# Gathering the first three tiles inside the routing block of a mixture-of-experts kernel, with part of the multiplications of zeros moved from the experts' block to the end of the routing

## The reference

```
x = x + 0.5 * ffn(layernorm(x))
x = x + attn(layernorm(x))
x = x + 0.5 * ffn(layernorm(x))
```

```
router_logits = x_flat @ gate_w                      # (2048, 8)
topk_w, topk_idx = top_k(softmax(router_logits), 2)
topk_w = topk_w / sum(topk_w)
x_rep_sort = x_flat[sort_idx // 2]                   # rows sorted by expert
h = silu(ragged_dot(x_rep_sort, w1)) * ragged_dot(x_rep_sort, w3)   # 256 -> 896
out_sort = ragged_dot(h, w2)                         # 896 -> 256
out = sum over the two experts of a token, weighted by topk_w
```

## Time and profile before

| what | value |
|---|---|
| median of 3 runs | 2851.32 us (2850.3 to 2853.34) |
| the profiled execution's own time | 2851.57 us |
| its span, first to last instruction | 2849.9 us |
| mean granted TensorE clock | 0.977 |
| TensorE (PE) busy | 2682.9 us, 94% |
| VectorE (DVE) busy | 1883.0 us, 66% |
| ScalarE (ACT) busy | 1357.7 us, 48% |
| GpSimd (POOL) busy | 692.1 us, 24% |
| DMA | 488.70 MB, mean 171 GB/s |

### The profile page before, as it was taken

The page is one execution under the profiler, slowest core; times in us unless marked ns, Lnnn a source line. Parts: engine busy times, 40 slices in busy tenths (PEclk is TensorE's granted clock), DMA queues, the critical chain, the costliest instruction groups (busy, mean ns, idle before and its releaser), DMA issues. The chain is left out here.

```text
span 2849.9 us, 63072 instructions
## 1 busy us (share of the span) xinstructions
PE 2682.9 (94%) x22216; PEld 2218.0 (78%) x22217; DVE 1883.0 (66%) x3550; ACT 1357.7 (48%) x4371; POOL 692.1 (24%) x969
## 2 busy tenths in 40 slices
PE   8999996748999999999999999999999997999997
PEld 7999995426777777777777777777777776899997
DVE  4111114979999999999999999999987544311111
ACT  1111112526666666666676666666665553011111
POOL 1222222421222222231322222231321111122221
PEclk8999998969999999999999999999999999999999
DMA  8777762555564554555554554546453322777674
GB/s 279 214 225 217 225 181 65 196 161 155 162 190 142 176 165 153 179 162 167 159 180 145 182 162 156 176 146 193 145 169 104 103 67 80 262 216 226 216 227 132
DMA packets 412292, 488.70 MB, mean 171 GB/s; under 512 B 215488, under 2 KB 295872, under 8 KB 412032
## 3 DMA queue, kind: packets, MB, share of 16 engines
q1 hardware_dynamic: 397056, 464.86, 50.4%
q0 software_dynamic: 14976, 20.46, 4.8%
HBM read 348.64 MB, written 138.67 MB: 171 GB/s over the span
## 5 line engine op out<-in xcount | busy, mean ns | idle before, releaser
L555 PE MATMUL f_ps_up<-f_xgT,f_w_up 128*128 128x128 f32 x4368 | 500.8, 275 | 0.0
L555 PEld LDWEIGHTS f_ps_up<-f_xgT,f_w_up 128*128 128x128 f32 x4368 | 494.4, 192 | 0.2
L624 DVE TENSOR_TENSOR f_hT<-f_hT,f_ps_up 128x512 f32<-128x512 f32 (+1 forms) x156 | 96.9, 621 | 503.4 <-ACT f_hT L603 503.4
L1574 DVE SCALAR_TENSOR_TENSOR at_qk<-at_bank,at_taps_qk,at_qk 128x510 f32<-128x510 f32 (+2 forms) x384 | 282.0, 744 | 36.1 <-ACT at_qk L1448 26.9
L1574 DVE SCALAR_TENSOR_TENSOR at_vT<-at_bank,at_taps_v,at_vT 128x510 f32<-128x510 f32 (+2 forms) x384 | 280.4, 744 | 35.9 <-ACT at_vT L1455 26.8
L603 ACT ACTIVATE f_hT<-f_ps_up 128x512 f32<-128x512 f32 (+1 forms) x156 | 84.9, 544 | 428.3 <-PE f_ps_up L555 428.3
L1844 POOL TENSOR_SCALAR at_small<-at_small 128x4 f32<-128x4 f32 x64 | 15.2, 238 | 1105.8 <-ACT at_squares L1482 1105.8
L1250 PE MATMUL at_bank<-xnT,at_w_qk 128*128 128x512 f32 x512 | 256.5, 625 | 11.7 <-DVE at_qk L1574 7.1
L519 POOL DMA_INDIRECT sums<-f_y,f_row_of x78 | 123.8, 1587 | 534.2 <-DVE f_y L630 534.2
L566 PE MATMUL f_ps_y<-f_w_down,f_hT 128*128 x1092 | 248.8, 379 | 3.8 <-DVE f_hT L624 3.8
L1275 PE MATMUL at_bank<-at_w_vz,xnT 128*128 128x256 f32 x1024 | 243.6, 381 | 8.5 <-DVE at_vT L1574 8.5
(11 more groups left out here) (230 smaller groups left out, 5535.1 us busy)
## 6 DMA issues: line engine op xcount, KB each, us to landing
f_w_up<-in_L_ffn_w_dram SPq DMA_DIRECT2D x156, 896.0 KB, 6.4
at_steps_e<-steps_kept SPq DMA_DIRECT2D x64, 512.0 KB, 6.9
mt_kept<-at_mt_made SPq DMA_DIRECT2D x64, 512.0 KB, 4.3
pt_kept<-at_pt_made SPq DMA_DIRECT2D x64, 512.0 KB, 3.1
at_mt<-mt_kept SPq DMA_DIRECT2D x64, 512.0 KB, 4.1
at_pt<-pt_kept SPq DMA_DIRECT2D x64, 512.0 KB, 4.6
qk_kept<-at_qk SPq DMA_DIRECT2D x64, 256.0 KB, 2.6
ks_kept<-at_ks_made SPq DMA_DIRECT2D x64, 256.0 KB, 2.7
```

The costliest lines, as they stand in the source:

```text
L555: last = te.matmul(ps_up[hf][w][:, at:at + P], w_up[b][:, w, k, P * j:P * j + P], xgT[b][:, k, :], start=(k == 0), stop=(k == KD - 1))
L624: v.tensor_tensor(part, part, ps_up[hf][1][:, 0:P * (high - low)], ALU.mult).then_inc(h_ready, 1)
L1574: ins = v_.scalar_tensor_tensor(out=dst[:, :, back:], in0=src[:, :, 0:SEQ - back], scalar=taps[:, 3 - back:4 - back], in1=dst[:, :, back:] ...
```

## The change

- The buffers `xg`, their semaphores `rows_loaded` and `gather` are defined for the whole of `build_ffn`. POOL issues the gathers of the first three tiles at the end of its program in the routing block, after waits for `rows_stored` (64) and for the second count of `table_ready`.
- TensorE multiplies zeros 9 times at the end of the routing block, and 6 times where it did 14 times at the start of the experts' block.
- In the experts' block POOL begins with the gather of tile 3. The order of its later gathers and stores is as before.

```diff
@@ -176,6 +176,15 @@
+        xg = [r.sb(f"xg{b}", [P, D]) for b in range(RING)]
+        rows_loaded = [r.dma_sem(f"rows_loaded{b}") for b in range(RING)]
+
+        def gather(t):
+            nc.gpsimd.indirect_dma_start(
+                out=xg[t % RING][:], out_offset=None, in_=rows_in,
+                in_offset=bass.IndirectOffsetOnAxis(ap=token_of[:, t:t + 1], axis=0),
+            ).then_inc(rows_loaded[t % RING], 16)
@@ -302,6 +311,7 @@
                     last.then_inc(tokens_summed, 1)
+                    keep_warm(nc.tensor, c, ps_logits[:, NT - D // EW:, :].rearrange("p t e -> p (t e)"), 9)
@@ -448,11 +458,14 @@
                     nc.gpsimd.tensor_copy(token[:], token_i[:]).then_inc(numbers_made, 1)
+                    pool.wait_ge(rows_stored, 64)
+                    pool.wait_ge(table_ready, 2)
+                    for t in range(RING):
+                        gather(t)
@@ -505,13 +517,6 @@
-                    def gather(t):
-                        at_least(pool, x_turned, t - RING + 1)
-                        nc.gpsimd.indirect_dma_start(
-                            out=xg[t % RING][:], out_offset=None, in_=rows_in,
-                            in_offset=bass.IndirectOffsetOnAxis(ap=token_of[:, t:t + 1], axis=0),
-                        ).then_inc(rows_loaded[t % RING], 16)
@@ -520,10 +525,10 @@
-                    for t in range(TILES):
+                    for t in range(RING, TILES):
+                        pool.wait_ge(x_turned, t - RING + 1)
                         gather(t)
-                        if t >= RING:
-                            store(t - RING)
+                        store(t - RING)
@@ -580,7 +585,7 @@
-                    keep_warm(te, c, spare[:, 0:D], 14)
+                    keep_warm(te, c, spare[:, 0:D], 6)
```

More of the change, by code:

```diff
@@ L454, in build_ffn @@
             q = Pools(nc, experts, prefix)
-            xg = [q.sb(f"xg{b}", [P, D]) for b in range(RING)]
             xgT = [q.sb(f"xgT{b}", [P, KD, P]) for b in range(RING)]
@@ L462, in build_ffn @@
             spare = q.ps("spare", [P, 512])
-            rows_loaded = [q.dma_sem(f"rows_loaded{b}") for b in range(RING)]
             rows_stored = [q.dma_sem(f"rows_stored{b}") for b in range(RING)]
```

## The result

| | before | changed |
|---|---|---|
| median | 2852.14 us (2848.31 to 2854.93, 12 runs) | 2857.66 us (2854.74 to 2860.39, 12 runs) |
| span of the profiled execution | 2849.9 us | 2855.9 us |
| TensorE busy | 2682.9 us | 2682.1 us |

The ratio is 1.0021, with a 95% interval of 1.0014 to 1.0029: slower by 4.0 to 8.3 us, 5.5 us between the medians. The forecast was slower, 2862.8 us, in a range of 2852 to 2869.

What follows compares the result with a forecast made beforehand. TensorE was taken to set the pace from each layer's first up; a later POOL DRAIN at the routing's end would delay these by 5.3 and 5.9 us, +11.2 us on 2851.57, giving 2862.8 us, range 2852 to 2869.

Steps and rivals of the forecast that it cites:

- What bounds the kernel, and by what path the change reaches the end: Experts' blocks: TensorE sets the pace, so each layer's first up, at 65.39 and 2462.09 us, shifts the end equally.
- SP's arrival unchanged, POOL's DRAIN the new last arrival, the clock down behind the moved zeros: Routing block's end: SP near 55 us, POOL's DRAIN from 0.6 to over 6 us, 12 records about 5.4 us.
- I take it as a fixed piece of time: POOL's DRAIN behind the routing's gathers: 6.42 us, as in the experts' block, whatever the number of DMAs; chance 0.53.
- I take the middle one, 64.0 and 2461.3: POOL's routing DRAIN ends at these times in the two layers, the fixed piece counted from the last gather issue's end.
- the DRAIN waits for the landing and little more: Rival at the routing's end: 0.08 us per DMA, 0.25 us for three; first ups +1.7 and +2.3, 2855.6 us; chance 0.30.
- the fixed DRAIN counted from its own start: Routing block's end: POOL's DRAIN ends at 61.5 us, first ups +2.8 and +3.4 us, 2857.8 us; chance 0.11.
- Issue of the gathers: POOL in the routing block: through issuing three gathers at 55.1 us, level with SP's 55.0; cost about 0.1 us.
- 6.4 us from a cold restart to the first up: Start of the experts' block: 12 records of zeros at half clock take 5.46 us, plus 0.92 us to the first up.
- The landing, 6.0 us beside the weight loads: Third gather in the routing block: lands 6.0 us after its issue, at 60.1 and 2457.4 us.
- The sum: Whole kernel: first ups +5.3 us in the first layer and +5.9 in the second, +11.2 us together, 2862.8 us.
- The faster rival: Routing block's end: POOL's DRAIN costs nothing of its own, clock stays up; first ups -6.4 and -5.8 us, 2839.4; chance 0.13.
- the gain of the rival that is faster comes from the zeros, not from them: Experts' block's start: moving the gathers brings nothing because they were hidden, landing by 64.9 us while TensorE multiplied zeros.

Runs made afterwards that it cites:

- experiment 6: Changed kernel with the w1 and w3 loads of the first three tiles moved from the routing block to the experts' block's start; 2859.95 us, one execution.
- experiment 1: Kernel before with 9 multiplications of zeros added at the routing's end and 15 instead of 14 in the experts' block, gathers unmoved; 2850.55 us, ratio 0.9996.
- experiment 9: Changed kernel with 21 instead of 9 multiplications of zeros behind the routing and none at the experts' block's start; 2847.00 us, ratio 0.9983.
- experiment 7: Changed kernel with only tile 0 gathered in the routing block, tiles 1 and 2 at the experts' block's start; 2849.72 us, ratio 0.9990.

## Why the prediction was right or wrong

- **What bounds the kernel, and by what path the change reaches the end: right.** The first up of each layer moved, and everything behind it with it.
- **SP's arrival unchanged, POOL's DRAIN the new last arrival, the clock down behind the moved zeros: right.** SP came at 55.2; the DRAIN grew from 0.6 to over 8 us; the clock stood at 0.50 from 58 on.
- **The failed step is "I take it as a fixed piece of time", with "I take the middle one, 64.0 and 2461.3".** The 6.42 us were 78 times 0.082 us, and the DRAIN behind three gathers ended 0.2 us after the third landing. Counted from the routing's last multiplication I had 13.2 us to POOL's arrival in both layers; it was 10.15 and 9.9. This term was 3.1 and 3.3 us too large. The two first ups were forecast 4.1 and 3.15 us too late, and it makes all of that but the 1.05 us of the restart below. The rival that the DRAIN waits for the landing and little more (given 0.30, and 2855.6 us) was the true one, and its tell, an experts' DRAIN shorter by 0.25 us, came as written. Its +1.7 and +2.3 us were measured as +1.2 and +2.75. That the fixed DRAIN counted from its own start gave 2857.8 us, next to the measured 2857.66, is a coincidence: there is no such piece.
- **Issue of the gathers:** priced level with SP at 55.1; they were through at 55.7, 0.6 us late by the first gather's 0.9 us behind its wait. This delays the third landing by as much.
- **"6.4 us from a cold restart to the first up":** 5.35 and 6.5 us. In the first layer the clock was up again from about 64.5, 3 us after the restart, where the earlier trace rows had shown 6.
- **The landing, 6.0 us beside the weight loads: right,** 6.0 and 5.9; experiment 6 shows that the loads make it so.
- **The sum:** +11.2 us forecast, +5.5 measured, on the right side and inside the range, close to the 0.2% that can be told from no change. The mechanism gives 1.2 + 2.75 - 0.25 = 3.7 us in the profile, a little under the interval of the runs (4.0 to 8.3). The rest of the profile's 6.1 us is one `down` at the half clock and 0.9 us between the layers, less 0.2 us at the end; since both wander from profile to profile with unchanged code, as told above, nothing here ties them to the change, and what the runs have above 3.7 us stays open. So the range was right and the mechanism behind its middle was not: that the measured time came as near to the forecast as it did is in part luck.
- **The faster rival fell,** since the DRAIN does wait. Its remark that "the gain of the rival that is faster comes from the zeros, not from them" is half right. The zeros alone gave 2.07 and 1.11 us (experiment 1) of its 6.4 and 5.8, up to the landing of the first gather. At an unchanged restart the zeros' place makes 4.3 and 5.3 us (experiment 9), of which 2.8 us in each layer are the 12 records that no longer stand behind the restart. But its first ups also come 1.1 and 1.4 us before those of experiment 1, whose clock was up as well and whose gathers were late: with the clock up, the early gathers do count.

## What to carry to other kernels

A block's end waits for each engine's DRAIN, and GpSimd's waits for its indirect DMAs to land and pays for every one issued since its last DRAIN: an early gather in front of such an end turns a transfer that was hidden into a wait for all engines. Put a DRAIN where GpSimd is idle anyway before a long list of indirect DMAs meets a barrier, and where a wait at a barrier can't be avoided, let TensorE multiply zeros through it rather than behind it.

## What the runs showed of the hardware that I had not expected

- POOL's DRAIN behind n indirect DMAs that have landed: 0.12 us for 1, 0.30 for 3, 0.54 for 6, 6.17 for 75, 6.34 for 77 (experiment 7), 6.42 for 78: about 0.05 + 0.082 n us. Where the landing came last, the DRAIN ended 0.17 us after it with three and 0.09 us with one.
- A gather of 128 rows of 1 KB landed 2.8 us after its issue with no weight loads beside it (DMA share 0.22 from 54 to 60.5 us of experiment 6) and 6.0 us after it beside 5.5 MB of them (share 0.99 from 52 to 61 us of the changed kernel).
- The first gather behind a wait of POOL started 0.90 us after the operation that released it in the first layer and 0.84 to 0.87 us after it in the second, in all ten kernels that gather in the routing block.
- After a standstill of 3.8 us the granted clock fell in one layer and held in the other of the same execution.
- TensorE's last `down` of a layer, behind an idle stretch of about 1.9 us, ran at the half clock (4.97 us) in 8 of the 26 layers and at the full clock (3.28 us) in the others.
